# Moving one round's row-number products behind the second expert's first up pair, in a three-layer decoder block

## The reference

```python
logits = xf @ Wr + br
Sm = softmax(logits, axis=-1)
G_t, idx_t = top_k(Sm.T, k)              # k = 2048 / 8 = 256 tokens for each expert
tokens = xf[idx]                          # gather
mid = silu(einsum('keh,ehf->kef', tokens, W_up[group]) + b_up[group])
out = einsum('kef,efh->keh', mid, W_down) + b_down
y = zeros_like(xf).at[idx].add(G[..., None] * out)   # scatter with addition
x = layernorm(x + y)
```

## Time and profile before

| what | us |
|---|---|
| median of 3 runs | 296.37 |
| the three runs | 293.88, 296.37, 305.04 |
| span of the profiled execution | 301.2 |
| PE busy in it | 249.7 (83%) |
| DVE, ACT, POOL busy in it | 193.8, 159.7, 137.8 |
| last run less the span | 3.8 |

### The profile page before, as it was taken

How to read it: one execution, slowest core, us unless ns; L and a number is a source line. 1 busy time by engine, 2 the same in 40 slices (tenths; PEclk the granted TensorE clock), 3 DMA queues, 4 the chain that set the end, 5 groups by cost and what they waited for, 6 DMA issues and landing times.

```text
span 301.2 us, 5168 instructions
## 1 busy us (share of the span) xinstructions
PE 249.7 (83%) x1689; PEld 205.1 (68%) x1689; DVE 193.8 (64%) x594; ACT 159.7 (53%) x336; POOL 137.8 (46%) x205
## 2 busy tenths in 40 slices
PE   8999999899988999999997111376599999999990
PEld 4756458575556879989895111336599999999890
DVE  1743357368957478848777788751267866776495
ACT  3654512525587356565324677212357987875454
POOL 6813955626253301555567976077453144443000
PEclk9999999999999799999999555557599999999998
DMA  6960013036192817469000399223226745522665
GB/s 185 291 139 16 1 31 77 0 70 139 32 209 64 181 42 150 114 164 307 4 1 1 111 394 291 86 73 108 71 55 160 204 71 113 125 33 26 159 218 209
DMA packets 33403, 35.59 MB, mean 118 GB/s; under 512 B 10338, under 2 KB 25698, under 8 KB 33122
## 3 DMA queue, kind: packets, MB, share of 16 engines
q1 hardware_dynamic: 29858, 30.90, 36.5%
q0 software_dynamic: 2784, 4.00, 7.8%
q10 hardware_dynamic: 736, 0.38, 0.4%
HBM read 18.16 MB, written 8.19 MB: 87 GB/s over the span
## 4 chain that ended last, share of the span: by engine, by line
PE 58%; DVE 16%; ACT 10%; issue 5%; DMA 4%; POOL 2%; another core or an unknown queue 2%; SPq 1%; DVEq 0%; POOLq 0%; ACTq 0%
PE bank L1218 13%; PE bank L1464 9%; PE bank L1675 6%; PE bank L1415 4%; DVE junk L2042 3%; PE bank L1307 3%; PE bank L1383 2%; PE bank L1451 2%; DMA Y<-summed_rows 2%; PE bank L1398 2%; ACT bank L1135 2%; PE bank L1427 1%; PE bank L1228 1%; DMA summed_rows<-OUT,idx 1%
## 5 line engine op out<-in xcount | busy, mean ns | idle before, releaser
L881 POOL DMA_INDIRECT summed_rows<-OUT,idx x14 | 21.8, 1556 | 37.8 <-DVE OUT L2160 35.7
L807 POOL TENSOR_SCALAR var_eps<-mean_var 128x1 f32<-128x1 f32 x32 | 7.3, 227 | 59.4 <-DVE mean_var L1886 59.0
L1464 PEld LDWEIGHTS bank<-VB,PT 128*128 128x128 f32 x256 | 33.0, 194 | 1.6
L1464 PE MATMUL bank<-VB,PT 128*128 128x34 f32 x256 | 31.4, 270 | 0.0
L1135 ACT ACTIVATE bank<-bank,b_up_c 128x256 f32<-128x256 f32 (+1 forms) x48 | 19.5, 447 | 18.1 <-PE bank L1218 13.0
L1218 PE MATMUL bank<-FTH,WUH 128*128 128x256 f32 x94 | 28.4, 302 | 0.0
L1218 PE MATMUL bank<-FTL,WUH 128*128 128x256 f32 x94 | 27.6, 293 | 0.0
L1218 PE MATMUL bank<-FTH,WUL 128*128 128x256 f32 x94 | 27.6, 293 | 0.0
L1893 DVE TENSOR_REDUCE NMF<-bank 128x8 f32<-128x512 f32 x32 | 21.7, 681 | 8.1 <-PE bank L1427 8.0
L1675 PE MATMUL bank<-WDH,MH 128*128 128x256 f32 x80 | 23.2, 290 | 1.2 <-DVE ML L2174 1.2
L871 POOL DMA_INDIRECT XG<-routed_rows,idx x16 | 15.5, 971 | 18.1 <-DVE idx L2136 13.8
(11 more groups left out here) (350 smaller groups left out, 743.4 us busy)
## 6 DMA issues: line engine op xcount, KB each, us to landing
WDR<-in_L_ffn_W_down SPq DMA_DIRECT2D x8, 640.0 KB
QS<-QH SPq DMA_DIRECT2D x32, 128.0 KB, 3.0
WUR<-in_L_ffn_W_up SPq DMA_DIRECT2D x4, 682.0 KB, 4.8
routed_rows<-X SPq DMA_DIRECT2D x2, 1056.0 KB, 10.0
X<-in_x SPq DMA_DIRECT2D x4, 512.0 KB, 5.1
QS<-QL SPq DMA_DIRECT2D x16, 128.0 KB, 3.0
summed_rows<-X SPq DMA_DIRECT2D x2, 1024.0 KB, 6.0
Y<-summed_rows SPq DMA_DIRECT2D x8, 256.0 KB, 5.5
```

The source lines that it names most:

```text
L881: pool.indirect_dma_start(summed, bass.IndirectOffsetOnAxis(ap=idx[:, 2 * e + h:2 * e + h + 1].bitcast(U32), axis=0), OUT[:, (2 * e + h) % ...
L1464: last = pe.matmul(o[:, j * 34:(j + 1) * 34], PT[m % 2][:, j, s * P:(s + 1) * P], VB[:, m // 2, j].rearrange("p h d -> p (h d)"), start=Tr ...
```

## The change

The row-number products of round 3, and the copy of their result, are moved from the step gt 1 (PE) and up 0 1 (DVE) to behind the step up 1 0 on both. The order of the banks' products follows. The slot products and `by_slot` stay.

```diff
@@ the order of the banks' products
-            if step == ("gt", 1):
+            if step == ("up", 1, 0):
                 product(("idx", PAIRS - 1), 3)
@@ PE
                 if (kind, *at) == ("up", 0, 1):
                     slot_numbers(PAIRS - 1)
-                if (kind, *at) == ("gt", 1):
+                if (kind, *at) == ("up", 1, 0):
                     row_numbers(PAIRS - 1)
@@ DVE
                 if step[0] == "up":
                     if step == ("up", 0, 1):
                         by_slot(PAIRS - 1)
+                    middle_low(*step[1:])
+                    if step == ("up", 1, 0):
                         by_row(PAIRS - 1)
-                    middle_low(*step[1:])
```

## The result

The changed kernel takes 299.62 us (median of 4 runs, 299.41 to 300.31); the kernel before, with one more run beside it, 295.38 us. The ratio is 1.015, 95% interval 1.0104 to 1.0197: slower, by 4.2 us between the medians. Executions that take several per cent longer at a lower granted clock, such as that of 305.04 us, are left out of every ratio, and without it the kernel before has 293.88, 294.40 and 296.37 us. The profiled execution has a span of 298.5 us and a time of 300.31 us, so 1.8 us lie around the span. The same holds in all later runs; the profiled execution of the kernel before, with its span of 301.2 us, thus took about 303.0 us (an estimate: 301.2 + 1.8), and not the 305.04 us that the table ahead of the prediction reads into it.

A forecast was written before the change was run, and what follows sets the result against it. PE was taken to set the pace through the experts. A 3.2 us wait for the bank plus 1.9 us of half clock gave +5.1 us on the median of 296.37: 301.5 us, range 297.0 to 306.5.

The forecast's parts named there:

- What goes at the old place: Between gt 1's transposes and up 0 2 on PE: gain of 0.3 to 0.57 us in the profiled execution, otherwise near nothing.
- late release: At 207 to 214 us, PE's results came up to 5.8 us behind their records; taken as neither gained nor lost.
- What comes at the new place: Dn 0 waits for bank 3 until DVE's copy, behind `ML`, `WUL`, `ML`: +3.2 us, bounds +2.6 to +3.8.
- The bank rule: Idx 3 and dn 0 become neighbours in bank 3, so emptying is exposed; the profile's row alone gave 0.14 us.
- Nothing overtakes, nothing soaks up: Work behind dn 0 waits with it; PE's later three waits, 1.2 us, absorb 0, at best 0.5 us.
- POOL: Round 3's gathers start near 221.9 instead of 214.85 and hold the first scatter at most 2 us: cost 0.
- The clock: PE's idle ahead of dn 0 brings the clock to half: +1.9 us, bounds 0 and 2.9 us.
- rival 1: Same wait ahead of dn 0 but no fall of the clock: 299.6 us, chance 0.15.
- a clock that stays full: Sign of being wrong: no half clock after PE's restart at dn 0, where 3 to 5 us were expected.
- Rivals 2 and 3: Late release of matmul results happens again, 302 to 307, say 304.5 us, chance 0.1; or it goes, 293.6 us, chance 0.08.

The follow-up runs named there:

- second comparison: The changed kernel run and profiled again with no further edit, against the kernel before: ratio 1.012 (1.0073 to 1.0168), lowest run 297.90 us.
- before's second profile: The kernel before, run and profiled again with no edit: ratio 1.001 (0.9974 to 1.0046), lowest run 294.17 us.
- other-bank kernel: The changed kernel with the row numbers of round 3 in bank 5 instead of 3: 294.57 us, ratio to before 0.9985 (0.9951 to 1.0019).
- copy behind `WUL`: The changed kernel with DVE's copy moved between `WUL` and `ML` of up 1 0: ratio to before 1.0083 (1.0048 to 1.0118).
- only the copy late: The changed kernel with PE's row products back at the old place behind gt 1, DVE's copy still late: 299.47 and 299.56 us, no ratio.

## Why the prediction was right

The direction, the wait for the bank and the range held; the forecast's 5.1 us stands against 4.2 and, in the second comparison, 3.5 us (1.2% of 295.8). The fall of the clock, which made up 1.9 of the 5.1 us, came in one profile of the changed kernel and not in the other.

- *What goes at the old place.* For an execution without the late release the prediction said near nothing, with `FTL` setting up 1 0. PE's wait of 0.36 us for `FTL` shows it. From the transposes to up 0 2 there are 0.71 us in before's second profile (206.54 to 207.25) and 0.41 us in the changed one (205.93 to 206.34); the 0.30 us gained are lost again at up 1 0. That A of the other-bank kernel is 0.17 us under before's (9.15 - 8.98) shows no gain either: its clock rose 0.8 us sooner within A.
- *What comes at the new place.* The order on DVE is as written: `ML`, `WUL`, `ML`, copy, dn 0. Against before's second profile A grows by 12.17 - 9.15 = 3.0 us in the first profile of the changed kernel and by 12.75 - 9.15 = 3.6 us in the second. With half of each stretch at half clock taken off (1.6, 2.2 and, for before, 2.0 us, an estimate from the windows above) both become 3.3 to 3.4 us, and PE's idle in A grows by as much (3.39 and 3.38 against 0.06). The prediction had 3.2 against the first profile of before and 3.4 to 3.8 for the case without the late release: the measured size lies at the lower end of the latter or just under it. One small assumption was wrong: dn 0's first matmul comes 0.26 us behind the copy's end and not 0.06.
- *The bank rule.* The Trainium skill's rule on rotating banks ("Perfetto Trace Analysis", "Optimizing Tensor Performance", Matmuls) was weighed against rows that showed no such wait. The other-bank kernel decides for the rule: one digit changed, and the whole loss of 1.2 to 1.5% came back.
- *Nothing overtakes, nothing soaks up.* B is 63.85 us before and 63.89 to 63.98 in the profiles without a fall: the three later waits of 1.2 us came along whole.
- *POOL.* Gathers 7 us later cost 0, and the first scatter was held by them, as said.
- *The clock.* This is the weak term. The forecast took a fall for the usual case (rival 1, "the clock holds", had 0.15) and priced it at +1.9 us. A fall costs 1.5 us, and it came in two of the three profiles with an unfilled idle of 3 us or more. It also came otherwise than the prediction had it: not in the idle, so that dn 0 starts at half clock, but 1.3 us behind the restart, for 3.4 us. In the second profile "a clock that stays full", one of the prediction's own signs of being wrong, is what happened. Where the clock fell, hole and fall make 3.4 + 1.5 = 4.9 us, close to the forecast's 5.1; where it held, 3.3 us. The run at a mean clock of 0.932, which the profiles without any such half clock also have (0.930 to 0.932 in before, the other bank and the copy behind `WUL`), is read as one of the latter kind: 297.90 us, against 294.38 and 294.66 us of the kernel before at 0.931 and 0.932, so +3.2 to +3.5 us. At 0.922 the mean clock does not tell which of the two it was: the second profile of the changed kernel (299.60 us, half clock at 97.5 us, no fall behind the hole) has 0.922, that with only the copy late (299.47 us, the other way round) 0.923. So how often the hole brought the clock down in the runs without a profile is open. That the median of 299.62 falls on rival 1's sum of 299.6 decides nothing: this sum starts from 296.37, a median of three runs with that of 305.04 us among them.
- *The late release.* Taken as neither gained nor lost, and it was absent on both sides. The profiled execution lay about 6.7 us above the median (303.0 less 296.37), not 8.67. Rivals 2 and 3, which needed it, got no support: it appeared in none of the eleven profiles taken since, with the row products directly behind fp32 products or far from them.

## What to carry to other kernels

When a small product is moved, follow its bank to the next owner and the copy that frees the bank to its place on the other engine: cost = (end of what is queued ahead of the copy) less (when the next owner would start), and the work that the product feeds may not matter at all. Count in what the other engine waits for on its way: of the 1.75 us of `WUL` only 0.6 us counted, as ACT was next late. An idle of 3 us can bring a fall of the clock on top, here 1.5 us in two profiles of three. If a result is not urgent, give it a bank whose next owner is not urgent either, or leave its copy ahead of long work such as the 1.75 us weight split. And take a second profile of the kernel before whenever the first one holds a piece that no engine owns.

## What the runs showed of the hardware

- The same program with the same 3.0 us idle of PE had its clock cut to half (1.2 GHz) 1.3 us after the restart in one execution and not at all behind that idle in another; one cut cost 1.5 us over the rest of the experts. The Trainium skill ("TensorE: Matmul & The Clock Gate", Part 1) says that the chip's watch on PE runs free of the kernel's start; two profiles that differ so agree with it, but they do not prove it.
- From the end of the copy into `idx` to dn 0's first matmul 0.26 us pass in every kernel with a hole (212.90 to 213.16, 210.67 to 210.93, 212.33 to 212.59, 213.20 to 213.46), against 0.06 us from `lh` to the row products in the kernel before. Why the one release is taken up so much later was not tried.
- In one execution PE's results reached ACT and DVE up to 5.8 us behind the recorded ends of their matmuls. It was seen once in twelve profiles, and its cause stays open.
